# Keys and values of layer 0: one Strassen product ahead of the loop in place of a projection in every slot

## The reference

```
x   = rmsnorm(hidden) * ln_weight
h_q = (x   @ w_q.T).reshape(b, lq, H, DH)
h_k = (ctx @ w_k.T).reshape(b, lk, H, DH)
h_v = (ctx @ w_v.T).reshape(b, lk, H, DH)
score = einsum('bqhd,bkhd->bhqk', h_q, h_k) + position_bias
p     = softmax(where(mask, score, -inf))
out   = hidden + einsum('bhqk,bkhd->bqhd', p, h_v).reshape(...) @ w_out.T
```

## Time and profile before

| | before |
|---|---|
| median of 3 runs | 1805.25 us (1804.73 to 1806.27) |
| span of the profiled execution, first to last instruction | 1802.2 us |
| PE busy | 1746.0 us (97%), 12080 matmuls |
| DVE, ACT, POOL busy | 1095.9, 790.4, 508.9 us |
| DMA | 65.95 MB, mean 37 GB/s |
| slots of layer 0 | from 9.75 us to 894 us |

### The profile page before, as it was taken

How to read it: one execution, slowest core, us unless ns; L and a number is a source line. 1 busy time by engine, 2 the same in 40 slices (tenths; PEclk the granted TensorE clock), 3 DMA queues, 4 the chain that set the end, 5 groups by cost and what they waited for, 6 DMA issues and landing times.

```text
span 1802.2 us, 31933 instructions
## 1 busy us (share of the span) xinstructions
PE 1746.0 (97%) x12080; PEld 1612.1 (89%) x12080; DVE 1095.9 (61%) x2008; ACT 790.4 (44%) x2171; POOL 508.9 (28%) x439
## 2 busy tenths in 40 slices
PE   6999999999999999999969999999999999999998
PEld 6889999999999999999858888888889898988887
DVE  7775555455455555556577657575666656575676
ACT  5333333333333333433314555555555555555553
POOL 2422222222222222221152333323333333233243
PEclk9999999999999999999989999999999999999999
DMA  5111101111011111011000100010010100010001
GB/s 211 50 51 51 39 13 51 51 51 40 20 44 51 50 51 39 13 51 36 24 24 24 36 13 24 24 35 23 23 35 13 45 10 25 23 35 15 1 1 48
DMA packets 23097, 65.95 MB, mean 37 GB/s; under 512 B 2768, under 2 KB 7248, under 8 KB 22992
## 3 DMA queue, kind: packets, MB, share of 16 engines
q1 hardware_dynamic: 22992, 64.40, 10.4%
HBM read 62.30 MB, written 2.10 MB: 36 GB/s over the span
## 4 chain that ended last, share of the span: by engine, by line
PE 90%; issue 4%; DVE 4%; POOL 1%; ACT 1%; DMA 0%; SPq 0%; POOLq 0%; DVEq 0%; ACTq 0%
PE bank L1288 26%; PE bank L1290 25%; PE bank L1289 25%; PE bank L1327 3%; PE bank L1534 3%; PE bank L1406 3%; PE bank L1553 2%; PE bank L1316 2%; PE bank L1435 1%; PE bank L1558 1%; DVE xt_lo L769 1%; DVE z_mid L779 0%; DMA ctx_stage<-ctx_t 0%; DVE stats L753 0%; PE bank L1303 0%
## 5 line engine op out<-in xcount | busy, mean ns | idle before, releaser
L403 POOL TENSOR_TENSOR work<-work,rn 128x512 f32<-128x512 f32 x64 | 66.7, 1042 | 661.5 <-DVE rn L887 661.5
L546 ACT ACTIVATE work<-work,nmax 128x128 f32<-128x128 f32 x256 | 99.8, 391 | 281.4 <-DVE nmax L872 281.4
L1288 PE MATMUL bank<-w_hi,ct_hi 128*128 128x256 f32 (+1 forms) x768 | 220.5, 287 | 2.3 <-issue 2.3
L1290 PE MATMUL bank<-w_hi,ct_lo 128*128 128x256 f32 (+1 forms) x768 | 214.9, 280 | 0.0
L1289 PE MATMUL bank<-w_lo,ct_hi 128*128 128x256 f32 (+1 forms) x768 | 214.9, 280 | 0.0
L1288 PE MATMUL bank<-w_hi,ot_hi 128*128 128x512 f32 (+1 forms) x512 | 212.9, 416 | 0.0
L1290 PE MATMUL bank<-w_hi,ot_lo 128*128 128x512 f32 (+1 forms) x512 | 201.4, 393 | 0.0
L472 POOL TENSOR_TENSOR p<-p,rn 128x512 f32<-128x512 f32 x128 | 131.2, 1047 | 244.1 <-DVE rn L1164 244.1
L1289 PE MATMUL bank<-w_lo,ot_hi 128*128 128x512 f32 (+1 forms) x512 | 199.7, 390 | 0.0
L1288 PE MATMUL bank<-w_hi,xt_hi 128*128 (+2 forms) x512 | 178.6, 349 | 0.0
L898 DVE TENSOR_TENSOR ot_lo<-bank,ot_hi 128x512 fp32r<-128x512 f32 x64 | 44.3, 692 | 215.9 <-ACT ot_hi L554 215.9
(11 more groups left out here) (154 smaller groups left out, 4716.0 us busy)
## 6 DMA issues: line engine op xcount, KB each, us to landing
stage<-w SPq DMA_DIRECT2D x99, 512.0 KB, 4.1
plain<-w SPq DMA_DIRECT2D x5, 512.0 KB, 3.5
ctx_stage<-ctx_t SPq DMA_DIRECT2D x4, 512.0 KB, 9.1
residual<-x SPq DMA_DIRECT2D x8, 256.0 KB, 8.0
bias_sb<-bias SPq DMA_DIRECT2D x16, 128.0 KB, 2.1
out<-residual SPq DMA_DIRECT2D x8, 256.0 KB, 2.0
stage<-ffn_w SPq DMA_DIRECT2D x1, 512.0 KB, 3.3
wl<-lnw SPq DMA_DIRECT2D x1, 256.0 KB, 6.4
```

Source lines behind the costliest of these rows:

```text
L403: pool.tensor_tensor(by4(pr), by4(pr), rn[:, :].unsqueeze(2).to_broadcast([P, 4, P]), ALU.mult).then_inc(norm_done, 1)
L546: last_op = nc.scalar.activation(by4(pr)[:, a, :], by4(sc)[:, a, :], ACT.Exp, bias=nmax[:, a:a + 1], accum_out=ssum[:, a:a + 1])
L1288: nc.tensor.matmul(out_ap, l_hi, r_hi, start=(c == 0), stop=False)
L1290: op = nc.tensor.matmul(out_ap, l_lo, r_hi, start=False, stop=(c == n - 1))
```

## The change

The keys and values of all heads are computed ahead of the slots, written to DRAM (`kd`, `vd`) and loaded back slot by slot into `kt` and `vs`. The product is a one-level Strassen product in Winograd's form: weights (halves of the output columns by halves of the 512 of contraction) and context (halves of the contraction by halves of the tokens) are cut into quarters, POOL and DVE form sums of quarters (S1 to S4 of the weights, T1 to T4 of the context), PE makes 7 products of quarters in place of 8, each with three passes, and ACT and DVE combine them.

The work is 32 **jobs**, in 8 steps of four: keys, values, keys, values. A job is 7 products. A product of keys is 6 matmuls of 512 columns (one group of two heads, half of the tokens as columns); one of values is 12 matmuls of 256 columns. Products are accumulated onto one another in a bank, so several wait until ACT has copied the partial sum out. Step 0 and step 7 are written out, the six between are one more hardware loop on every engine. All 1024 tokens of a job's keys or values (1 MB) lie in `kout` or `vout`, one buffer each, until they are stored.

In a slot, K and V are gone from PE and their copies from ACT; the weight splits fall from four to two in a group (q and o); `probabilities_out` goes from DVE to ACT (`probabilities_copied`). PE runs the scores first, and the queries one slot ahead: S of slot j, TP of j-1, Q of j+1, AV of j-1, OP of j-2.

```
+            def products_early(s, k):
...
+                wait(pe, c12_done, job - 1)
+                product(1, k, 0, True).then_inc(product_done, 1)
...
+                wait(pe, c11_done, job - 1)
+                product(2, k, 1, True).then_inc(product_done, 1)
+            def products_middle(s, k):
...
+                pe.wait_ge(part1_done, job + 1)
+                product(6, k, 0, False).then_inc(product_done, 1)
...
+                product(7, k, 2, True).then_inc(product_done, 1)
...
+                pe.wait_ge(part2_done, job + 1)
+                product(5, k, 0, False).then_inc(product_done, 1)
+            def products_last(s, k):
...
+                pe.wait_ge(part4_done, job + 1)
+                product(3, k, 0, False).then_inc(product_done, 1)
+                pe.wait_ge(c22_done, job + 1)
+                product(4, k, 2, False).then_inc(product_done, 1)
+            def projections(s):
...
+                for k in range(4):
+                    products_early(s, k)
+                    if k > 0:
+                        products_last(s, k - 1)
+                    elif not first:
+                        products_last(s - 1, 3)
+                    products_middle(s, k)
...
+            def part1(s, k):
+                job = 4 * s + k
+                wait(act, (kd_out, vd_out)[k % 2], 16 * (2 * s + k // 2))
+                act.wait_ge(product_done, nth(1, job))
+                nc.scalar.activation(job_out(k, 0, 0), job_bank(k, 0), ACT.Copy).then_inc(part1_done, 1)
...
+            def quarter21(s, k):
+                dve.wait_ge(product_done, nth(4, 4 * s + k))
+                dve.wait_ge(part2_done, 4 * s + k + 1)
+                nc.vector.tensor_tensor(job_out(k, 1, 0), job_out(k, 1, 0), job_bank(k, 2), ALU.add).then_inc(c21_done, 1)
...
+            def store_keys(s, half_s):
+                all_quarters(4 * s + 2 * half_s)
+                sp.dma_start(kd[2 * s + half_s, :, :, :], kout[:, :, :, :].rearrange("p m n t -> p m (n t)")).then_inc(kd_out, 16)
...
+            def load_keys(t, j):
...
+                sp.dma_start(kt[:, j % 2, :].rearrange("p (h n) -> p h n", h=2),
+                             kd[2 * t + j // 4, :, :, 256 * (j % 4):256 * (j % 4 + 1)]).then_inc(kt_in[j % 2], 16)
...
+                if not (last and j == BODY - 1):
+                    masked_bias(t + (j + 1) // BODY, (j + 1) % BODY)
+                if first and 1 <= j < 1 + B // 2:
...
+                pool.wait_ge(rn_done, i + 1)
+                pool.tensor_tensor(by4(pr), by4(pr), rn[:, :].unsqueeze(2).to_broadcast([P, 4, P]),
+                                   ALU.mult).then_inc(norm_done, 1)
```

More of the change, by code:

```diff
@@ L262, in some_high, with nth @@
             return eng.value_load(flag[0:1, 0:1], min_val=0, max_val=1)
+        quarter = lambda full, k, n: full[:, 2 * k:2 * k + 2, 512 * n:512 * (n + 1)]
+        T1, T2, T3, T4 = range(4)
+        def nth(product, job):
+            if isinstance(job, int) and job <= 0:
+                return (1, 2, 8, 9, 5, 3, 4)[product - 1] if job == 0 else 0
+            if isinstance(job, int) and job == 4 * SG - 1 and product in (3, 4):
+                return 7 * job + 3 + product
+            return 7 * job + (-1, 0, 8, 9, 5, 3, 4)[product - 1]
@@ L323, in _ @@
+            for j in range(BODY):
+                slot(0, j)
+            with sp.Fori(1, TL - 1) as t:
+                for j in range(BODY):
+                    slot(t, j)
+            for j in range(BODY):
+                slot(TL - 1, j)
+            for piece, used, count in ((2, w_lo_done[1], NG), (0, q_ps, U - 4), (1, y_ps, U - 4), (3, added, U), (4, s_ps, U)):
                 sp.wait_ge(used, count)
@@ L383, in _, with projections @@
+            def projections(s):
+                last = isinstance(s, int) and s == SG - 1
+                weight_sums(kraw, kraw_in, ksum_done, 2 * s + 1)
+                if not last:
+                    weight_sums(vraw, vraw_in, vsum_done, s + 1)
+                    weight_sums(kraw, kraw_in, ksum_done, 2 * s + 2)
+            projections(0)
+            with pool.Fori(1, SG - 1) as s:
+                projections(s)
+            projections(SG - 1)
+            for p in range(4):
                 row_roots(0, p)
@@ L548, in exponentials, with probabilities_copied @@
                 last_op.then_inc(exp_done, 1)
+            def probabilities_copied(count):
+                act.wait_ge(pt_ps, count)
+                wait(act, o_ps, count - 1)
+                nc.scalar.activation(ptr, TB[:, :], ACT.Copy).then_inc(pt_done, 1)
             def output_hi(count, j):
@@ L624, in _ @@
             weight_hi(1)
-            exponentials(U)
             weight_hi(2)
@@ L964, in slot @@
                 else:
-                    for k in range(2):
-                        dequantise(2 * (TL - 2 + k) + j // 4, j % 4, BODY * (TL - 2) + 2 * j + k + 1)
+                    dequantise(2 * (TL - 1) + j // 4, j % 4, BODY * (TL - 2) + 2 * j + 2)
+                if last and j == BODY - 1:
+                    dve.wait_ge(acc_done, U - 3)
+                    row_stats(1, 0)
             for j in range(BODY):
@@ L1656 @@
         "gates": gates,
+        "wk0": quarters(a["L0_xattn_w_k"], NG),
+        "wv0": quarters(a["L0_xattn_w_v"], SG),
         "w0": w0,
```

832 lines of the change are left out of this document (545 added, 287 removed).

## The result

| | before | after |
|---|---|---|
| median of the runs | 1805.39 us (4 runs, 1804.73 to 1806.27) | 1761.39 us (4 runs, 1761.12 to 1762.73) |
| ratio | | 0.9759, 95% interval 0.9746 to 0.9772 |
| profiled execution | span 1802.2 us, its time is not on record | span 1759.3 us, time 1761.12 us |

The change saves 44.0 us; predicted were 1760 and a range of 1744 to 1787. The sum lands within 1.4 us, but only because errors of either sign cancel, as the parts show, and 3.5 of the 44 us are not the product's at all. In every run for which both are on record the time lies 1.8 to 1.9 us above the span. So the profiled execution of the kernel before took some 1804.0 us (an estimate), 1.2 us less than its median; the 3.05 us that the forecast counts between span and time are 1.2 too many.

The account below looks back on a forecast made before the run. PE was taken to bound the kernel, with 90% of the last chain. Shared point 363 + 477 + 5.5 + 0.5 + 2.7 = 849 against 894: span 1802.2 - 45 = 1757, plus 3.05 gives 1760 us; range 1744 to 1787.

Parts of the forecast that it names:

- Start: From the kernel's begin until nine of 224 products are done: at 33 us, bounds 28 to 38.
- the lower bound: Start of the kernel: 28 us if ACT gets part2 before the late weights' sums are ready.
- the upper bound: Start of the kernel: 38 us if DVE is later by a few splits.
- Projections: Product stage ahead of the slots: 215 products in 300 us, plus 1.4 transposes and 4.5 stalls, ending at 339.
- Passage: Last product to the slots: S(0) ends 7.8 us behind it, TP(1) comes 24.1 behind it, at 363.
- Slots: Layer 0 from TP(1) on: 7.76 us a slot bound by PE, 477 in sum; first body 5.5 more.
- Shared point: PE's first transpose of the feed-forward weight, code unchanged behind it: at 849 against 894, 45 us earlier.
- Stores: Product stage: a 1 MB store lands in 4 to 5 us, hidden, as it has 8.1 us.
- Turns: PE's loops: if body size decides, all issue gaps at the turns go, 9.8 us in layer 0 before.
- Turns do cost: Rival, PE's loops: every turn costs, 2 us each, +10 to +20, giving 1770 to 1780; 20%.
- The slot stays PE's: Against the rival for layer 0's slots that DVE bounds them: 8.3 us for 7.76, 33 us lost, 1793; 13%.
- Late stores: Rival, product stage: each us beyond 8.1 costs 30 jobs 1 us each; at 10 us landing 1817, slower; 8%.

Follow-up runs that it names:

- no_first_sums: Changed kernel without POOL's four sums of the values' weights for step 0, their places zeroed: 1754.43 us, ratio 0.9716.
- start_order: Changed kernel with only the order of ACT and DVE at the start changed, part1 and part2 taken earlier: 1755.56 us, ratio 0.9731.
- passage_order: Changed kernel with slot 0's exponentials and maxima taken ahead of weight splits on ACT and DVE: 1755.90 us, ratio 0.9736.
- stores_thrice: Changed kernel with every store issued three times, to three DRAM tensors, and all waits for all three: 1837.51 us, ratio 1.0180.
- The kernel before, padded: Kernel before with four small SBUF tensors added, so that everything allocated behind them lies at other addresses: 1791.00 us, ratio 0.9924.
- eight_products: Changed kernel with the second of each job's seven products issued twice, so eight products a job: 1804.15 us, ratio 0.9991.

## Why the prediction was right, step by step

- **Start: 33 forecast, 40.0 measured, the step that failed.** It was outside its bounds of 28 to 38. P1 came at 8.36, not at 9.75, which changed nothing, since P6 waits for part1 (20.6, forecast 20.3). Part2 ended 5.8 us late, at 30.6 for 24.8: the sum went along ACT's list alone and put POOL's sums (four of 2.1 to 2.3 us, done at 26.8) at nothing, though part2 stands behind them on ACT; they appear only in the lower bound. no_first_sums and start_order show it from either side. The other 1.2 us are the clock behind P5's wait, 2.3 us where 1 was counted. DVE's splits, named for the upper bound, took 2.3 to 2.6 us each and held nothing here.
- **Projections: 215 products in 300 us forecast.** From 40.03 to the last matmul's end near 344.8 are 304.75 us with the transposes, where 300 + 4.5 + 1.4 = 305.9 were counted. The 4.5 us of stalls did not come (one wait of 0.31 us); a product of keys took 1.37 to 1.40 and one of values 1.42 to 1.44 us, not 1.37 and 1.42, some 3 us in all. Two errors cancel in part.
- **Passage:** S(0) ends 5.9 us behind the last product (7.8 forecast), TP(1) starts 22.3 behind it (24.1). The wait for the second q weight, named in the forecast, is what holds it: passage_order takes 4 us out.
- **Slots:** 7.81 us instead of 7.76, 3 us in 61 slots; no engine but PE bounds them. DVE is busy for 5.8 us and ACT for 3.8 of a slot (6.0 and 3.9 forecast). The first body is some 4.5 us longer than steady slots would be (ACT's copies of seven slots, 367.73 to 426.93, against 7 x 7.81; 5.5 forecast); leaving out DVE's unpack gives 3.8 of them back.
- **Shared point:** 854.80; the sum of the forecast, unrounded, is 363 + 477 + 5.5 + 0.5 + 2.7 = 848.7. The errors are +7.0 (start), -1.2 (projections), -1.8 (passage), +2.0 (slots and tail), in sum +6.0 of the 6.1 us.
- **Layer 1:** -3.5 us, not forecast, most of it from addresses (moving them back returned 2.4). "Behind it nothing is changed" was true of the code and false of where its operands lie. This took 3.5 of the 6.1 us back, and the 1.2 us too many between span and time took another part: 6.1 - 3.5 - 1.2 = 1.4 us. So the parts are right in their mechanism but for the start, and that the total is so near is luck.
- **Stores:** 4.4 and 4.8 us to land, 4 to 5 forecast, slack 8.1 as forecast. **Turns:** no gap in either new loop, as forecast.
- **The rivals:** none came true. Turns do cost, in bodies beyond a size that the new ones don't reach. The slot stays PE's. Late stores would make the kernel slower than before, as stores_thrice does at 1837.51.

One thing stands beside the 44 us. The kernel before, padded, takes 1791.00 us. Against that version the change saves 1791.00 - 1761.39 = 29.6 us, and eight_products is 13 us slower than it: so the stage ahead of the loop, with its start and passage, seems to have a price of its own, which the old kernel's slow addresses and turns hid, and the saved eighth pays it. Its parts were not measured apart. The padded kernel still has its gaps at the turns (8.9 us); padded and written out it would take about 1782 us (an estimate, not run), and the change would save some 21 us of that. How much of the change's 39 us in layer 0 comes from the addresses alone was not separated, since its layer 0 has another layout at either address.

## What to carry to other kernels

When a stage is pulled ahead of a loop, follow the first job through every queue, with each engine's durations taken beside the engines that will really run then: on ACT what stands behind a wait counts more than its own work. A one-buffer store is safe up to a slack that can be computed, and beyond it a wait of PE can cost a stretch of slow clock besides its length. And before a few us are credited to an algorithm, shift the buffers by 128 bytes: here that alone made 14 us.

## What the runs showed of the hardware

- 128 bytes of shift in SBUF, same instructions: 14.2 us of 1805 in one kernel, 2.4 of 1761 in the other; single matmuls differ by 2 to 4 ns. Which relation of addresses does it stays open: only two positions were tried.
- DVE's 128x1024 subtraction took 1.21 to 1.23 us with POOL at rest and mostly 1.75 to 2.6 beside POOL's sums; POOL's 128x512 sums took 1.3 us with DVE nearly at rest (no_first_sums, from 43.46 us) and 2.1 to 2.3 beside the splits.
- In stores_thrice a wait of 2.3 us on PE in a full stage was followed by some 3.3 us at the level of 1.2 GHz, one of 3.31 us was not; over the stage, 47.5 us of waits cost 70.
- Bodies of 448 and 640 matmuls turn without a gap, 832 with two, 896 with one a turn; why 896 costs less than 832 was not found.
